# Attention scores per head on 32-row strips: 64-key blocks in place of block-diagonal keys

## The reference

```python
x = x + attn(layernorm(x))      # 16 heads of 8 values; q, k, v = x @ w_in.T + b_in
                                # scores = q . k / sqrt(8), allowed where j <= i and j >= i - 128
                                # softmax over j, times v, then @ w_out.T + b_out
x = x + ffn(layernorm(x))       # 16 experts of width 64, grouped top-4 routing, and a shared expert
```

## Time and profile before

| | |
|---|---|
| median of 3 runs | 893.09 us (893.0 to 902.63) |
| profiled execution | 893.77 us, its span 892.1 us |
| TensorE busy | 802.1 us (90%) |
| VectorE, ScalarE, GpSimd busy | 640.4, 408.1, 173.3 us |
| mean granted TensorE clock | 0.958 |
| transfers | 45.9 MB, 51 GB/s over the span |

### The profile page before, as it was taken

One profiled execution on the slowest core, in us unless ns is written; L12 is line 12 of the kernel. 1 busy time (PEld: TensorE's weight loads), 2 busy tenths in 40 slices (PEclk: granted clock), 3 DMA queues, 4 the chain that ended last, 5 costly groups with the idle time before them and its releaser, 6 DMA issues.

```text
span 892.1 us, 26601 instructions
## 1 busy us (share of the span) xinstructions
PE 802.1 (90%) x9713; PEld 589.8 (66%) x9713; DVE 640.4 (72%) x2037; ACT 408.1 (46%) x765; POOL 173.3 (19%) x290
## 2 busy tenths in 40 slices
PE   3399898898997989979988799999999999999998
PEld 2277677676876768767777566666666666666664
DVE  6867677676785867858773677777787777777774
ACT  2266566565674757647666233223223222233222
POOL 7412111120112201221111211222222122211200
PEclk9589899998999989989999799999999999999999
DMA  4222112220222122221120111100111111110000
GB/s 127 61 75 86 41 49 87 86 78 24 74 86 86 40 63 73 86 66 56 54 86 14 60 36 36 35 23 12 35 35 35 35 35 35 35 35 24 24 13 12
DMA packets 53323, 45.90 MB, mean 51 GB/s; under 512 B 10976, under 2 KB 42992, under 8 KB 53232
## 3 DMA queue, kind: packets, MB, share of 16 engines
q1 hardware_dynamic: 53232, 44.50, 16.5%
HBM read 27.44 MB, written 17.04 MB: 50 GB/s over the span
## 4 chain that ended last, share of the span: by engine, by line
PE 76%; DVE 11%; issue 6%; ACT 4%; DMA 2%; SPq 0%; POOL 0%; DVEq 0%; ACTq 0%; POOLq 0%
PE ps_c L1518 12%; PE ps_att L1334 10%; PE ps_sc L1311 5%; PE ps_max L1500 4%; PE ps_max L1502 4%; PE ps_max L1501 4%; PE ps_att L1510 4%; PE ps_max L1283 4%; PE ps_sc L1501 3%; PE ps_sc L1502 3%; PE ps_sc L1500 3%; DVE chunkmax L885 3%; PE ps_b L1239 2%; PE ps_c L1362 2%; PE ps_b L1348 2%
## 5 line engine op out<-in xcount | busy, mean ns | idle before, releaser
L775 ACT ACTIVATE kdiag<-ps_max 128x512 f32<-128x512 f32 x144 | 86.0, 597 | 223.9 <-PE ps_max L1502 184.8
L885 DVE TENSOR_REDUCE chunkmax<-ps_max 128x16 f32<-128x512 f32 (+1 forms) x256 | 155.2, 648 | 40.9 <-PE ps_max L1265 40.9
L688 ACT ACTIVATE probs<-ps_sc 128x512 f32<-128x512 f32 (+1 forms) x256 | 132.1, 568 | 78.0 <-PE ps_sc L1265 77.8
L1334 PE MATMUL ps_att<-probs,vdiag 128*64 128x160 f32 (+4 forms) x2048 | 122.6, 273 | 3.3 <-ACT probs L688 3.1
L1518 PE MATMUL ps_c<-kdiag,wd 128*128 128x512 f32 x256 | 125.4, 592 | 0.0
L1334 PEld LDWEIGHTS ps_att<-probs,vdiag 128*64 128x64 f32 x2048 | 115.3, 138 | 11.1 <-ACT probs L688 7.3
L1311 PE MATMUL ps_sc<-qstack,kdiag 128*128 128x160 f16 (+4 forms) x1024 | 97.1, 223 | 23.4 <-issue 22.9
L1311 PEld LDWEIGHTS ps_sc<-qstack,kdiag 128*128 128x128 f16 x1024 | 69.3, 100 | 45.7 <-issue 35.9
L1113 DVE TENSOR_TENSOR kdiag<-kdiag,ps_sc 128x512 f32<-128x512 f32 x128 | 87.3, 682 | 12.6 <-PE ps_sc L1502 8.4
L1121 DVE TENSOR_TENSOR kdiag<-kdiag,ps_att 128x512 f32<-128x512 f32 x128 | 87.2, 682 | 10.7 <-PE ps_att L1510 7.0
L1283 PE MATMUL ps_max<-hl,qdiag 32*128 32x160 f16 (+4 forms) x1024 | 50.7, 219 | 33.4 <-DVE chunkmax L885 26.6
(11 more groups left out here) (153 smaller groups left out, 1420.7 us busy)
## 6 DMA issues: line engine op xcount, KB each, us to landing
qk_scratch<-hl SPq DMA_DIRECT2D x32, 256.0 KB, 2.4
...
```

The lines of the kernel that those rows point to most:

```text
L688: nc.scalar.activation(probs[s % 4][:, at:at + BANK_COLS[h]], ps_sc[h][:, 0:BANK_COLS[h]], ACT.Exp, scale=SCALE).then_inc(probs_ready, 1)
L775: nc.scalar.activation(silu[slot][rows, :], ps_max[slot][rows, :], ACT.Silu).then_inc(silu_ready, 1)
L885: nc.vector.tensor_reduce(chunkmax[:, 2 * pair + m, at:at + CHUNKS[h]], ps_max[m][:, 0:BANK_COLS[h]].rearrange("p (n k) -> p n k", k=KB), ...
L1334: last = mm(ps_att[64 * gi:64 * gi + 64, gp * S + q0:gp * S + q0 + width], vdiag[p][:, (b * NB + m) * G + g, :], probs[(2 * u + gi) % 4][: ...
```

## The change

- `kdiag` and `spread_k` are gone. `kstack` exists twice, and `qstack` and `kstack` hold each head in a strip of 32 rows: 8 rows of each of three parts, one row for the maxima. `store_split` loads them with 24 transfers of 8 rows instead of 6 of 32.
- `scores(u)`, u = 0 to 9, five per sequence: units 0 to 3 hold the products of four heads with three 64-key blocks (12 products, one head per 32-row strip, output 64 keys by up to 192 queries), the fifth the last key block of all 16 heads (16 products of 64 queries). Every unit fills both banks, and waits until both were read. Masks are `mask2`, 64 rows each.
- Probabilities lie per pair of heads in `probs` (8 tiles) and `tails` (2 tiles). `attend(b, half)` multiplies them in four 32-column tiles (12 products), `attend_tails(b)` adds the last key block (8 products).
- `vdiag` has half the size. `project_v` computes 64x64 outputs, 4 products a part. `spread_v` has two copies instead of four.
- The lists of TensorE and ScalarE are written anew around this. The buffers of the feed-forward half (`spare`) no longer share memory with `kdiag`.

Old lines of `scores` and `attend` are not repeated here, they stand in the listing above.

```diff
+    TB = 64
+    NKB = S // TB
+    PAIRS = H // 2
+    UNITS = 2 * (C + 1)
+    QCOLS = [min(3 * TB, S - TB * m) for m in range(NKB)]
...
-        kstack = sb("kstack", [P, G, TOK], FP16)
-        kdiag = [sb(f"kdiag{p}", [P, G, 2 * NB, C, KB], FP16) for p in range(2)]
-        vdiag = [sb(f"vdiag{p}", [P, 2 * NB * G, 64], FP32) for p in range(2)]
+        kstack = [sb(f"kstack{p}", [P, G, TOK], FP16) for p in range(2)]
+        vdiag = [sb(f"vdiag{p}", [P, 2 * NKB * PAIRS, 32], FP32) for p in range(2)]
...
-        probs = [sb(f"probs{n}", [P, COLS], FP32) for n in range(4)]
+        probs = [sb(f"probs{n}", [P, 512], FP32) for n in range(PAIRS)]
+        tails = [sb(f"tails{n}", [P, 4 * TB], FP32) for n in range(2)]
...
-        spare = kdiag[0][:, :, :, :, :].rearrange("p g n c k -> p (g n c k)").bitcast(FP32)
+        spare = sb("spare", [P, 8 * TOK], FP32)
...
-                for t, part in enumerate((0, 1, 0)):
-                    sp.dma_start(qstack[p][32 * t:32 * t + 32, :, :],
-                                 hl_d[p, :, part, 0, :].rearrange("(g r) t -> r g t", g=G)
-                                 ).then_inc(qk_loaded[p], 16)
-                if i.begun:
-                    sp.wait_ge(kdiag_act, i.count(1, 0))
-                if i.begun:
-                    sp.wait_ge(kdiag_dve, i.count(1, 0))
-                for t, part in enumerate((0, 0, 1)):
-                    sp.dma_start(kstack[32 * t:32 * t + 32, :, :],
-                                 hl_d[p, :, part, 1, :].rearrange("(g r) t -> r g t", g=G)
-                                 ).then_inc(qk_loaded[p], 16)
+                for stack, n, parts in ((qstack[p], 0, (0, 1, 0)), (kstack[p], 1, (0, 0, 1))):
+                    for t, part in enumerate(parts):
+                        for r in range(C):
+                            sp.dma_start(stack[32 * r + HD * t:32 * r + HD * t + HD, :, :],
+                                         hl_d[p, :, part, n, :].rearrange("(g r d) t -> r d g t", g=G, r=C)[r]
+                                         ).then_inc(qk_loaded[p], 16)
...
-            def exps(i, s):
-
-                act.wait_ge(pv_done, i.lag(4, s // 2 - 1))
-                for h in range(2):
-                    act.wait_ge(sc_full, i.lag(16, 2 * s + h + 1))
-                    at = h * BANK_COLS[0]
-                    nc.scalar.activation(probs[s % 4][:, at:at + BANK_COLS[h]], ps_sc[h][:, 0:BANK_COLS[h]],
-                                         ACT.Exp, scale=SCALE).then_inc(probs_ready, 1)
+            def exps(i, u):
+
+                b, r = u // (C + 1), u % (C + 1)
+                act.wait_ge(pv_done, i.lag(6, 3 * b + (r // 2 - 2 if r < C else 0)))
+                for s in range(2):
+                    act.wait_ge(sc_full, i.lag(2 * UNITS, 2 * u + s + 1))
+                    dst = probs[2 * r + s] if r < C else tails[s]
+                    nc.scalar.activation(dst[:, :], ps_sc[s][:, 0:dst.shape[1]], ACT.Exp, scale=SCALE
+                                         ).then_inc(probs_ready, 1)
...
@@ body(i), ScalarE @@
                 exps(i, 3)
-                take_att(i, 0)
                 exps(i, 4)
                 exps(i, 5)
+                take_att(i, 0)
+                exps(i, 6)
                 take_attn(i, 0)
-                if prep:
-                    spread_k(i, 0)
-                    spread_k(i, 1)
-                exps(i, 6)
                 exps(i, 7)
+                exps(i, 8)
                 if prep and not (i.j is None and i.c + 1 >= STEPS):
                     transpose_out(i.next())
-                if prep:
-                    spread_k(i, 2)
+                exps(i, 9)
                 take_att(i, 1)
-                if prep:
-                    spread_k(i, 3)
                 take_attn(i, 1)
...
@@ prep_attn(i, prep, attn), VectorE @@
                 if prep:
                     row_maxima(i, 0)
                     chunk_maxima(i, 4)
-                    spread_k(i, 0)
-                    spread_k(i, 1)
                     chunk_maxima(i, 5)
                 if attn:
                     add_residual(i, 0)
                 if prep:
-                    spread_k(i, 2)
                     chunk_maxima(i, 6)
-                    spread_k(i, 3)
                 if attn:
...
-                wv = wT[:, 2, :].rearrange("p (g c d) -> p c g d", g=G, c=C)
-                for n in range(part * NB // 2, (part + 1) * NB // 2):
-                    for c in range(C):
-                        last = mm(ps_a[32 * c:32 * c + 32, n * 32:(n + 1) * 32].rearrange("p (g d) -> p g d", g=G),
-                                  xT[:, n * KB:(n + 1) * KB], wv[:, c], start=True, stop=True,
-                                  tile_position=(0, 32 * c))
+                wv = wT[:, 2, :].rearrange("p (n e d) -> p e n d", n=PAIRS, e=2)
+                for n in range(part * NKB // 2, (part + 1) * NKB // 2):
+                    for e in range(2):
+                        last = mm(ps_a[TB * e:TB * e + TB, n * TB:(n + 1) * TB].rearrange("p (n d) -> p n d", d=HD),
+                                  xT[:, n * TB:(n + 1) * TB], wv[:, e], start=True, stop=True,
+                                  tile_position=(0, TB * e))
...
+            def mask2(s, cols, edge):
+
+                rows = slice(TB * s, TB * s + TB)
+                n = (cols.stop - cols.start) // TB
+                return mm(ps_sc[s][:, cols].rearrange("p (n k) -> p n k", n=n),
+                          repeat2[rows, :, :].rearrange("p e k -> p (e k)"),
+                          edges2[rows, edge, :].unsqueeze(1).to_broadcast([TB, n, TB]),
+                          start=False, stop=True, skip_group_check=True, tile_position=(TB * s, 0))
+
+            def scores(i, u):
+
+                b, j = u // (C + 1), u % (C + 1)
                 p = 1 - i.parity
+                if u == 0:
+                    pe.wait_ge(qk_loaded[p], i.next(-1).half(16 * 24, 16 * 24))
+                if j == 0:
                     pe.wait_ge(max_loaded[b], i.count(16, 0))
+                pe.wait_ge(probs_ready, i.lag(2 * UNITS, 2 * u))
+                pieces = [(j, m) for m in range(NKB - 1)] if j < C else [(jj, NKB - 1) for jj in range(C)]
+                for at, (jj, m) in enumerate(pieces):
+                    q0 = b * S + TB * m
+                    for r in range(C):
+                        s, e = r // 2, r % 2
+                        rows = slice(32 * r, 32 * r + 32)
+                        dst = ps_sc[s][TB * e:TB * e + TB, :].rearrange("p (n k) -> p n k", k=TB)
+                        dst = dst[:, at::NKB - 1, :][:, 0:QCOLS[m] // TB, :] if j < C else dst[:, at:at + 1, :]
+                        mm(dst, kstack[p][rows, jj, q0:q0 + TB],
+                           qstack[p][rows, jj, q0:q0 + QCOLS[m]].rearrange("p (n k) -> p n k", k=TB),
+                           start=(at == 0), stop=False, skip_group_check=True, tile_position=(32 * r, TB * e))
+                if j < C:
+                    for s in range(2):
+                        mask2(s, slice(0, 3 * TB), 0)
+                    for s in range(2):
+                        mask2(s, slice(6 * TB, 8 * TB), 1).then_inc(sc_full, 1)
+                else:
+                    for s in range(2):
+                        mask2(s, slice(0, 4 * TB), 0).then_inc(sc_full, 1)
+
+            def attend(i, b, half):
+
                 p = 1 - i.parity
+                pe.wait_ge(probs_ready, i.lag(2 * UNITS, 2 * (b * (C + 1) + 2 * half + 2)))
+                if b == 0 and half == 0:
                     pe.wait_ge(vdiag_ready, i.count(1, 0))
+                if half == 0:
                     pe.wait_ge(attT_ready, i.lag(2, b))
+                for m in range(NKB - 1):
+                    n = QCOLS[m] // TB
+                    for x in range(4):
+                        pair = 4 * half + x
+                        last = mm(ps_att[32 * x:32 * x + 32, half * S + TB * m:half * S + TB * m + QCOLS[m]
+                                         ].rearrange("p (n k) -> p n k", k=TB),
+                                  vdiag[p][:, (b * NKB + m) * PAIRS + pair, :],
+                                  probs[pair][:, :].rearrange("p (n k) -> p n k", k=TB)[:, m::NKB - 1, :][:, 0:n, :],
+                                  start=(half == 0 and m == 0), stop=(m == NKB - 2), skip_group_check=True,
+                                  tile_position=(0, 32 * x))
+                last.then_inc(pv_done, 1)
+
+            def attend_tails(i, b):
+
+                p = 1 - i.parity
+                pe.wait_ge(probs_ready, i.lag(2 * UNITS, 2 * (b + 1) * (C + 1)))
+                for half in range(2):
+                    for x in range(4):
+                        pair = 4 * half + x
+                        j, s = pair // 2, pair % 2
+                        last = mm(ps_att[32 * x:32 * x + 32, half * S + 3 * TB:half * S + 4 * TB],
+                                  vdiag[p][:, (b * NKB + NKB - 1) * PAIRS + pair, :],
```

(47 more changed lines are left out.)

147 lines of the change are left out of this document (54 added, 93 removed).

## The result

The changed kernel takes 1017.1 us (median of 4 runs, 1014.0 to 1021.8), the kernel before 897.9 us beside it (4 runs, 893.0 to 903.9): ratio 1.1345, 95% interval 1.129 to 1.140. The ratio is taken over executions in the faster of the chip's two states, so it is not quite the quotient of the two medians. The forecast was 967 us, range 928 to 1010: the direction held, the size did not. The profiled execution took 1021.8 us, its span is 1019.8.

The account below looks back on a forecast made before the run. The prediction took the order of work and the waits between engines, not TensorE's work alone, to bound the attention step. Profiled 893.8 + 15 x 3.7 (steps) - 6 (start) + 3 (last step) + 4 (table loads) + 17 (clock) = 967 us, range 928 to 1010.

Parts of the forecast that it names:

- The step at the full clock: One attention step, from one project_qk to the next: 25.8 us before, 29.5 us after, +3.7.
- The parts: Four stretches of a step, split at scores(3), transpose_att(0) and the next attend: 7.4, 6.55, 4.05 and 11.5 us.
- TensorE's stall: Third part of a step: TensorE stands still 3.0 us at score_maxima(5), waiting for chunk_maxima(4) behind normalise(0).
- The clock: The 3.0 us stall drops the granted clock in about 6 of 15 steps, +2.8 us each, +17 in all.
- First part: Step's start to scores(3): unchanged at 7.4 us, as the wait for VectorE's first chunk_maxima ends it.
- the start: Kernel start and first step: smaller vdiag memsets and no kdiag work, together about -6 us (bounds -8 and -2).
- the expert half: Feed-forward loop: ScalarE's table load at the head of each of 7 passes costs 0.6 us, +4 us.
- step 15 with the last one: Last step: one exchange more and a table load before the last exponentials, +3 us (1 to 5), besides a step's +3.7.
- Loads in a row: Rival: weight loads of the scores units run one after another, +3.0 us a step, 1012 us; chance 0.12.
- Waits half hidden: Rival: only the exchanges between scores and exponentials cost, the maxima are not held up, 907 us; chance 0.07.
- TensorE-bound: Rival: TensorE's work is the bound and its shorter products count in full, 833 us; chance 0.07.
- SP's queue: Rival: SP's 24 loads end the step if an issue takes over 0.6 us; at 0.7 about 985 us; chance 0.04.

Follow-up runs that it names:

- e10: The changed kernel in its own order, with 20 unused products a step (5, 12 and 3 at three places): 964.2 us.
- e6: e3 plus 5 unused products of 512 columns ahead of score_maxima(1) at the step's head: 935.6 us.
- e7: e3 plus scores written bank by bank and the last exps ahead of the expert scores, saving table loads: 1018.5 us.
- e12: e3 plus expert tables loaded once, 11 unused products a step and 5 more: 912.5 us, ratio 1.013 to 1.029 against the kernel before.
- e5: The changed kernel with scores written one bank after the other, two heads at a time: 1138.1 us.
- e3: The changed kernel with row_maxima(0) and chunk_maxima(4) ahead of normalise(0) on VectorE: 962.7 us.
- e4: The kernel before, with its own tiles, in the order of the change: 989.7 us.

## Why the prediction was wrong

**The step at the full clock: right.** Forecast 29.5 us, 29.78 in e10; the 14 steps of e10 are 3.87 us longer than before, forecast +3.7. The parts were 7.40, 6.48 and 4.31 us for 7.4, 6.55 and 4.05 (4.10 in e10, where the clock has not yet fallen at their end), the fourth 11.81 for 11.5, TensorE's stall 3.04 for 3.0. The mechanism was as told: the transposes started 1.5 us after `chunk_maxima(3)` had ended, and the maxima behind `normalise(0)` ended the wait.

**The clock: the mis-sized term.** "So the new stall of 3.0 us should drop it in about 6 of 15 steps ... +17 in all (0 to 42)". It was 53 us. What failed is the count of the falls, in two ways. I took the six loop ends as a sample, three of which dropped the clock within 3.0 us (the others 3.3 to 4.1 us after the last product, not 3.1 to 3.8), and read it as a chance of a little under a half. In all 14 steps the clock fell in or right behind the stall, or was low already. And loop ends were the wrong sample: they come after dense work, while the new stall follows a head of the step in which TensorE waits 0.38, 1.60 and 0.66 us as well, and in six steps the clock fell within 1.0 us of the stall's start, sooner than at any loop end of before (1.7 us). And I priced one place. Eleven falls began 7 to 12 us into a step, where this change took work from TensorE without making VectorE's maxima any earlier. I wrote "First part: unchanged, 7.4", which is right at the full clock; but the wait of 0.64 us there grew to 1.60, and e6 shows that filling this alone gives 27 us. The trace of before held the sign: its fall at 196.0 lies at this place. So there were 27 falls in the 14 steps in place of 7, where the forecast had 6 more. The price of 2.8 us each looks right (53 us over 20 more falls is 2.65), but partly by luck: it was worked out from some 5 us at half clock, and the falls last 8.2 us on average, part of which waits hide.

**The sum with it.** 893.8 + 55.5 - 6 + 3 + 4 + 53 = 1003; measured 1017 (median) and 1022 (profiled). Nearly all that is left lies outside the 14 steps: the start gave -5.9 as forecast, the expert half +9.4 instead of +4 (a table load costs 1.1 us a pass, e7, not 0.6; the other 1.7 us are within the spread of the runs, since e12, without the loads, takes 392.9 us there and the kernel before 393.6), and step 15 with the last one +16.7 instead of +6.7, of which e10 takes away 4.5 with its clock; the other 5.5 us stay open.

**Single sizes.** Twelve products of a unit took 0.34 us (302.04 to 302.39) as taken, four masks 0.25 (forecast 0.18). A tail unit's 16 products, of 64 queries each, took 0.25 (303.87 to 304.12), 16 ns each and not the 28 taken from the others. `attend` halves 1.01 (0.96), their tails 0.36 (0.21). `project_v` took 0.38 us a part, the same as before with a quarter of the instructions (forecast 0.10): at 48 ns each, fewer instructions bought nothing. By these sizes TensorE's work fell by about 2.2 us a step, an estimate, where I had 4.1. That is small beside the clock: TensorE was waiting anyway. Its busy share in the 14 steps was 75% (89% before), not two thirds, half-clock time counted in.

**The rivals.** Loads in a row (1012 us) came closest to the measured time and is false: a product takes 28 ns, and 16 in the tail units, not 57. The Trainium skill (TensorE: Matmul & The Clock Gate, Packing small matmuls, The mechanism) lets a weight load overlap the products in flight when its row strip is another one; the 28 and 16 ns with four strips agree. The 57 ns with two in e5 are a price of its order, of the strips or of the single bank. Waits half hidden and TensorE-bound are out by the 3.04 us. SP's queue: its 24 loads were issued in 8.2 us, at 0.34 us each, below the forecast 0.44, and e3 with the same queue is 54 us faster; it does not end the step.

**Which part of the change costs.** Its order, put on the old tiles (e4), costs 93 us; taking back one piece of order on VectorE (e3) gives 54. These are not shares of the 120 us, since order and tiles meet in the clock. At the full clock the order explains the step: e4's last one would take some 30.4 us (31.88 less about 1.4 for its one fall, an estimate), e10's takes 29.78, that of before 25.8. Beyond that the clock was low for 94 us in e4 and for 224 in the changed kernel, whose tiles leave TensorE less busy. With VectorE's order mended (e3) 1.1 us a step are left at the full clock, of tiles, exchange and the rest of the order together. No run has the new tiles in the order of before, so the tiles' own share is not shown.
